# Who rescales the running sums in a graph attention layer: VectorE or GpSimd

## The reference, cut to what matters

```python
q = (h @ Wq + bq).reshape(n, NUM_HEADS, HEAD_DIM) * scaling
k = (h @ Wk + bk).reshape(n, NUM_HEADS, HEAD_DIM)
v = (h @ Wv + bv).reshape(n, NUM_HEADS, HEAD_DIM)
s = jnp.einsum('ehd,ehd->eh', q[row], k[col])
m = jax.ops.segment_max(s, row, num_segments=n)
p = jnp.exp(s - m[row])
denom = jax.ops.segment_sum(p, row, num_segments=n)
attn = p / denom[row]
out = jax.ops.segment_sum(attn[:, :, None] * v[col], row, num_segments=n)
return out.reshape(n, HIDDEN) @ Wo + bo
```

## Time and profile before

| | us |
|---|---|
| median of 3 runs | 8501.01 |
| lowest and highest run | 8488.27, 8502.29 |
| span of the profiled execution | 9608.8 |
| steady part of the changed loop in it | 6100 to 8080 |

### The profile page before, as it was taken

The page is one execution under the profiler, slowest core; times in us unless marked ns, Lnnn a source line. Parts: engine busy times, 40 slices in busy tenths (PEclk is TensorE's granted clock), DMA queues, the critical chain, the costliest instruction groups (busy, mean ns, idle before and its releaser), DMA issues. The chain is left out here.

```text
span 9608.8 us, 121761 instructions
## 1 busy us (share of the span) xinstructions
PE 6035.1 (63%) x27004; PEld 3698.3 (38%) x27227; DVE 5624.6 (59%) x14481; ACT 2416.0 (25%) x7255; POOL 5956.5 (62%) x5564
## 2 busy tenths in 40 slices
PE   2121155555555555547999997899999997554544
PEld 0010033333333333334444444555555555333333
DVE  4100055555555555556888887899999998222224
ACT  0000033333333333322333332344444443000000
POOL 5777655555555555546888884566666665666663
PEclk6555566666666666668999998999999999667676
DMA  1000032223222232322332333344444444333334
GB/s 64 1 10 10 17 88 83 83 78 83 81 80 80 81 83 78 81 55 73 85 84 85 84 84 52 111 120 119 119 119 121 120 119 101 90 90 89 89 90 55
DMA packets 405871, 777.59 MB, mean 81 GB/s; under 512 B 195938, under 2 KB 225356, under 8 KB 405196
## 3 DMA queue, kind: packets, MB, share of 16 engines
q0 software_dynamic: 279488, 712.60, 28.4%
q1 hardware_dynamic: 126348, 64.59, 2.3%
HBM read 736.75 MB, written 40.07 MB: 81 GB/s over the span
## 5 line engine op out<-in xcount | busy, mean ns | idle before, releaser
L495 POOL DMA_INDIRECT rec_s<-wts,rows x784 | 780.5, 995 | 1085.2 <-ACT rows L467 870.5
L1829 POOL DMA_INDIRECT gat<-y,rec_sb_s x892 | 1182.5, 1326 | 298.0 <-issue 278.8
L2098 POOL DMA_INDIRECT gat<-x,rec_sb_d x892 | 846.5, 949 | 484.5 <-issue 266.2
L965 POOL DMA_INDIRECT gat<-kv,rec_sb_d x896 | 906.7, 1012 | 334.7 <-issue 272.9
L1381 POOL DMA_INDIRECT gat<-kv,rec_sb_s x900 | 861.5, 957 | 398.5 <-issue 313.9
L2113 PE MATMUL ps<-gat,oh 128*128 128x256 f32 x1760 | 648.5, 538 | 680.2 <-DVE acc L2133 253.6
L1577 DVE TENSOR_REDUCE small<-ps 128x2 f32<-128x1024 f32 x884 | 1041.7, 1216 | 6.9 <-PE ps L1445 5.7
L434 POOL DMA_INDIRECT rec_d<-small x784 | 810.7, 1034 | 343.0 <-issue 265.1
L1870 PE MATMUL ps<-big,oh 128*128 128x512 f32 x1760 | 947.3, 637 | 0.0
L2113 PEld LDWEIGHTS ps<-gat,oh 128*128 128x128 f32 x1760 | 462.9, 274 | 865.5 <-issue 497.1
L1048 PE MATMUL ps<-big,oh 128*128 128x264 f32 x1768 | 754.1, 541 | 0.3
(11 more groups left out here) (276 smaller groups left out, 13129.7 us busy)
## 6 DMA issues: line engine op xcount, KB each, us to landing
gat<-kv,rec_sb_s POOLq DMA_INDIRECT x900
gat<-kv,rec_sb_d POOLq DMA_INDIRECT x896
rec_sb_s<-rec_s SPq DMA_DIRECT2D x448, 32.0 KB, 2.2
gat<-y,rec_sb_s POOLq DMA_INDIRECT x892
gat<-x,rec_sb_d POOLq DMA_INDIRECT x892
rec_d<-small POOLq DMA_INDIRECT x784
rec_s<-wts,rows POOLq DMA_INDIRECT x784
rec_s<-gat SPq DMA_DIRECT2D x4, 1808.0 KB, 16.7
```

Source lines behind the costliest of these rows:

```text
L495: e.indirect_dma_start(out=recs["s"], out_offset=bass.IndirectOffsetOnAxis(ap=pr[:, t:t + 1], axis=0), in_=rr[:, t, :], in_offset=None).th ...
L965: e.indirect_dma_start(out=gat[:, m.u, q, :], out_offset=None, in_=table, in_offset=bass.IndirectOffsetOnAxis(ap=r_sb[:, m.u, q, 0:1].bitc ...
L1829: e.indirect_dma_start(out=rows_y[m.u][:, q, :], out_offset=None, in_=y1, in_offset=bass.IndirectOffsetOnAxis(ap=r_sb[:, m.u, q, 0:1].bitc ...
L2098: e.indirect_dma_start(out=gat[:, m.u, q, 0:D], out_offset=None, in_=x3, in_offset=bass.IndirectOffsetOnAxis(ap=r_sb[:, m.u, q, 0:1].bitca ...
```

## The change

In the loop of the second attention layer three things move. `rescale` goes from VectorE to GpSimd: in each turn GpSimd first rescales the sums of macro `M(-1)`, then weights the values of `M(0)`, then gathers; it loads the bucket number into a register for that. The first macro has no rescale ahead of it (`pool_first`). The write-back of the running maximum goes from VectorE to ScalarE, as a copy behind the two exponentials, with a bucket load of its own on ScalarE. A new semaphore `kept` counts these copies, and VectorE waits for the copy of the macro before ahead of taking the new maximum. VectorE signals `f` with L1595, and the internal waits that kept L1593 ahead of the write-back are gone. `add_sums` still waits for `rs`, now from GpSimd.

```diff
--- before.py
+++ after.py
@@ -1328,7 +1328,7 @@
         def attention_by_node(table):
 
             s = stages("a2", "far", "oh", "tr", "oht", "qx", "prod", "s3", "st", "sp", "mq", "me", "f", "ef", "p",
-                       "pv", "sum", "rs", "flush")
+                       "pv", "sum", "rs", "flush", "kept")
             s_hm, s_hr = sem("a2_hm"), sem("a2_hr")
             credits.append((s_hr, 3))
             s_rec = [sem(f"a2_rec{u}") for u in range(U)]
@@ -1364,6 +1364,12 @@
             r = recs["s"].rearrange("(p m q) w -> m p (q w)", p=P, q=Q)
 
 
+            def bucket(e, m):
+                return e.value_load(jmap["s"][0:1, bass.ds(m.index(), 1)], min_val=0, max_val=NB - 1)
+
+            def by_head(j):
+                return acc[:, bass.ds(j, 1), :].rearrange("p a (h c) -> p (a h) c", c=HC)
+
             def load_record(e, m):
                 at = e.snap(m.index())
                 e.wait_ge(s["prod"], m.done(U))
@@ -1391,18 +1397,30 @@
                 G.tensor_tensor(pw[:, :, :, 0:DH], gv, pw[:, :, :, DH:HC].to_broadcast([P, Q, H, DH]),
                                 ALU.mult).then_inc(s["pv"], 1)
 
-            def pool_turn(e, M):
+            def rescale(e, m):
+                at = by_head(bucket(e, m))
+                e.wait_ge(s["ef"], m.done())
+                e.wait_ge(s["flush"], m.done(1))
+                G.tensor_tensor(at, at, bcast(ff[m.v], 2, [P, H, HC]), ALU.mult).then_inc(s["rs"], 1)
+
+            def pool_first(e, M):
                 weight_values(e, M(0))
                 gather(e, M(U))
 
+            def pool_turn(e, M):
+                rescale(e, M(-1))
+                weight_values(e, M(0))
+                gather(e, M(U))
+
             def pool(e):
                 G.memset(acc, 0.0).then_inc(S("zeroed"), 1)
-                macro_loops(U, gather, pool_turn, start=1)(e)
+                for m in range(U):
+                    gather(e, Macro(0, m))
+                pool_first(e, lambda lag: Macro(0, lag))
+                macro_loops(0, None, lambda e, M: pool_turn(e, lambda lag: M(1 + lag)))(e)
                 all_landed(e, every_gather)
 
 
-            def bucket(e, m):
-                return e.value_load(jmap["s"][0:1, bass.ds(m.index(), 1)], min_val=0, max_val=NB - 1)
 
             def turn_one_hots(e, m):
                 e.wait_ge(s["oh"], m.done())
@@ -1510,11 +1528,13 @@
                 A.activation(st3[m.v][0:24, :], scores, ACT.Copy).then_inc(s["sp"], 1)
 
             def exponents(e, m):
+                j = bucket(e, m)
                 e.wait_ge(s["f"], m.done())
                 e.wait_ge(s["sum"], m.done(2))
                 A.activation(pvb[:, m.v, :, :].rearrange("p q (h c) -> p q h c", c=HC)[:, :, :, DH],
                              v4(sm), ACT.Exp).then_inc(s["p"], 1)
                 A.activation(ff[m.v], dd, ACT.Exp).then_inc(s["ef"], 1)
+                A.activation(m_run[:, bass.ds(j, 1), :], mn, ACT.Copy).then_inc(s["kept"], 1)
 
             def scalar_turn(e, M):
                 keep_scores(e, M(1))
@@ -1554,15 +1574,6 @@
                 c.wait(k)
                 V.tensor_tensor(t[:, :, 2, :], t[:, :, 1, :], top(t[:, :, 1, :]), ALU.subtract).then_inc(s["s3"], 1)
 
-            def by_head(j):
-                return acc[:, bass.ds(j, 1), :].rearrange("p a (h c) -> p (a h) c", c=HC)
-
-            def rescale(e, m, j):
-                e.wait_ge(s["ef"], m.done())
-                e.wait_ge(s["flush"], m.done(1))
-                V.tensor_tensor(by_head(j), by_head(j), bcast(ff[m.v], 2, [P, H, HC]), ALU.mult)\
-                    .then_inc(s["rs"], 1)
-
             def add_sums(e, m, j):
                 e.wait_ge(s["rs"], m.done())
                 e.wait_ge(s["sum"], m.done())
@@ -1581,20 +1592,17 @@
                 jz = None if start else bucket(e, z)
                 maxima(1)
                 split_scores(c, e, M(1), k_sc)
-                if not start:
-                    rescale(e, z, jz)
                 maxima(2)
                 maxima(3)
                 mj = m_run[:, bass.ds(ja, 1), :]
                 e.wait_ge(s_hr, a.i * (U * PAIRS) + (a.off * PAIRS + PAIRS + 3))
+                e.wait_ge(s["kept"], a.done(1))
                 V.tensor_tensor(mn, mj, mx, ALU.max).then_inc(s["mq"], 1)
                 multiply(e, M(2))
                 e.wait_ge(s["mq"], a.done())
-                k_dd = c(V.tensor_tensor(dd, mj, mn, ALU.subtract))
+                V.tensor_tensor(dd, mj, mn, ALU.subtract)
                 e.wait_ge(s["me"], a.done())
-                c(V.tensor_tensor(v4(sm), s3[a.u][:, :, 0, :], v4(at_edge), ALU.subtract))
-                c.wait(k_dd)
-                V.tensor_scalar(mj, mn, 1.0, None, ALU.mult).then_inc(s["f"], 1)
+                V.tensor_tensor(v4(sm), s3[a.u][:, :, 0, :], v4(at_edge), ALU.subtract).then_inc(s["f"], 1)
                 k_sc = take_scores(c, e, M(2))
                 if not start:
                     add_sums(e, z, jz)
@@ -1617,7 +1625,7 @@
                 multiply(e, Macro(0, 1))
                 k_sc = take_scores(cc, e, Macro(0, 1))
                 vector_turn(cc, e, lambda lag: Macro(0, lag), k_sc, start=True)
-                first, per = cc.n, 4
+                first, per = cc.n, 2
                 e.wait_ge(S("zeroed"), 2)
 
                 def turn(e, M):
```

## The result

Beside the kernel before on one chip, the changed kernel took 8534.94 us (median of 4 runs, 8529.03 to 8538.67) against 8497.3 us (4 runs): ratio 1.0047, 95% interval 1.0035 to 1.0059. That is +38 us where -9 was forecast. The time lies inside the stated range, and it moved the other way; the prediction's chances had leaned to slower (0.34 against 0.28 for faster) while its sum named a gain.

What follows compares the result with a forecast made beforehand. TensorE and VectorE, both 93% busy, were read as two equally long branches before pair 3's reduce. Terms -0.03 - 0.08 + 0.07 = -0.04 us a turn, times 220 = -9 us, gave 8492 us, range 8418 to 8560.

Steps and rivals of the forecast that it cites:

- Rescale on GpSimd: GpSimd's slot between last gather and weighting: 0.63 us rescale after a 0.30 us gap fits, add does not wait.
- Rival B: GpSimd's rescale holds VectorE's difference of maxima, 0.65 us more in 66 turns: +42 us, 8543 us; chance 0.16.
- Rescale off VectorE: Between split and pair 3's reduce: rescale hidden beside TensorE's branch, gain 0.02 to 0.07 us a turn, 0.03 taken.
- Write-back off VectorE: Behind the difference at the edges: the reduce of the products starts sooner, 0.08 us less a turn.
- the new wait: VectorE's wait "kept" ahead of the new maximum: never late, handling costs 0 to 0.09 us a turn, 0.07 taken.
- hidden rescale: VectorE's rescale before pair 3's reduce runs beside an equally long TensorE branch; removal gains 0.03 us a turn.
- A: VectorE sets the pace, so the rescale's 0.35 us a turn comes out in full: -79 us, 8422 us; chance 0.10.
- C: GpSimd's turn becomes the longest, 9.29 us, and the add waits for the rescale: +55 us, 8556; chance 0.16.
- D: TensorE's late release at the edges changes: -83 us (8409), chance 0.07, or +36 us (8528), chance 0.04.

Runs made afterwards that it cites:

- e6: Kernel before plus an idle GpSimd multiply of 128x264 on spare SBUF ahead of each weighting, nobody waiting for it; ratio 1.0076.
- e7: Kernel before plus an idle GpSimd memset of 128x264 on spare SBUF ahead of each weighting; ratio 1.0000.
- e5: Kernel before with the rescale of the running sums left out on every engine; ratio 0.9997.
- e15: Kernel before with only the write-back and its wait moved to ScalarE, rescale left on VectorE, 8494 us chip; ratio 0.9974.
- e9: The whole change, unchanged, run again beside the kernel before on the 9415 us chip; ratio 1.0037.
- e8: Kernel before, unchanged, profiled again on the 9415 us chip; ratio 1.0006.
- e11: Kernel before with only the write-back and its wait moved to ScalarE, rescale left on VectorE, 9415 us chip; ratio 0.9998.
- e0: Kernel before, unchanged, profiled again on the 9602 us chip; ratio 1.0000.

## Why the prediction was wrong, point by point

**The step that failed is "Rescale on GpSimd", in its cost to VectorE.** It checked whether GpSimd has room and whether the add has to wait, found both harmless, and set the instruction at nothing. Both findings hold for the usual turn: the rescale took 0.64 us (0.63 forecast), GpSimd still waited 0.55 us for ScalarE in 204 of 217 turns, and the add waited in 9. But the instruction was costly to an engine that doesn't wait for it: 151 holds of 0.28 us, 42 us in all. Rival B had the mechanism, the place and the sign, at 0.16, and gave 8543 us against 8535 measured. The error was in the weighing. I set it back because no row of before shows a two-input subtract beside a GpSimd multiply. None could: GpSimd had no multiply in that slot before, and in the whole loop none of VectorE's instructions with two SBUF inputs ran beside the weighting. And the sum put the two within 0.02 us of each other.

The Trainium skill, SBUF — State Buffer, states in section Who interferes with whom that a VectorE instruction with two SBUF inputs contends with a GpSimd instruction that reads SBUF, and in section SBUF: two separate sides that the one that starts first keeps the shared ports for its whole length. The runs agree where a GpSimd multiply started first: L1603 ends 0.03 us behind the rescale in all 151 turns (6009.28 and 6009.25 above), and e6 does the same with an idle multiply. Whether a GpSimd instruction that only writes would hold VectorE is barely told by the few turns of e7.

**Rival B's own sum was right by two errors.** It took 0.65 us in 66 turns. Measured: the gap between gather and rescale is 0.02 us, not the 0.30 chosen from gather to gather, so the rescale ends sooner and the hold is 0.28 us where it happens (L1603 0.44 instead of 0.16 us). But it happens in 151 of 221 turns, and on the timed chip L1605 has no wait for TensorE under which a hold could hide. 151 x 0.28 = 42 us, where B had 0.65 x 66 = 43. That its total came within 8 us of the measured time is luck.

**"Rescale off VectorE" was right.** 0.02 to 0.07 us a turn was forecast, 0.03 taken. The wait at pair 3 in after shows it, and the 3 us of e5 are 0.01 a turn, between -0.02 and 0.05 by the interval.

**"Write-back off VectorE" was right in size, the new wait too dear.** After has 0.10 us from L1605 to L1567 (9.21 to 9.31) against 0.19 from L1595 to L1547. The wait "kept" was set at 0.07 us; of the 217 turns 54 pay it, 12.7 us as L1600's wait for L1588, 0.24 us each against the 0.15 that is there anyway: 0.09 x 54 / 217 = 0.02 in the mean. Together -0.07 to -0.10 us a turn on an 8500 us chip, where e15 measured -22 us; the forecast had -0.01.

**What the sum left out: long turns.** Nine times in the loop, in every kernel, GpSimd's second gather of a macro starts 2.02 us behind the end of the first instead of 0.30. Without the rescale on GpSimd its idle time takes that up on an 8500 us chip: in e5 and e15 the turns with such a gather are at most 0.15 us longer than their neighbours of the same place. In after the rescale stands between these gathers and VectorE's add:

```profile
6021.20 0.99 POOL L1387 DMA_INDIRECT gat<-kv,rec_sb_s  x1 [0.80 <-issue]
6024.20 0.95 POOL L1387 DMA_INDIRECT gat<-kv,rec_sb_s  x1 [2.02 <-issue]
...
6027.67 0.64 POOL L1404 TENSOR_TENSOR acc<-acc,small 128x264 f32 x1
```

```profile
6024.94 0.17 DVE L1600 TENSOR_TENSOR small<-m_run,small 128x8 f32<-128x8 f32 x1
...
6028.46 0.43 DVE L1580 TENSOR_TENSOR acc<-acc,ps 128x264 f32 x1 [0.87 <-POOL acc L1404]
...
6035.26 0.58 DVE L1600 TENSOR_TENSOR small<-m_run,small 128x8 f32<-128x8 f32 x1 [0.24 <-DVE small L1588]
```

That turn is 6035.26 - 6024.94 = 10.32 us. Four of the nine are of this kind, where the loop closes, and five take 9.54 us in the third place. Against e5's turns in the same places (8.67 and 8.58) that is 4 x 1.65 + 5 x 0.96 = 11 us, 0.05 a turn. L1603 is not held in them. I looked at mean slack (rows of a usual turn) where the rare gap decides. The row was there to be read, in the waits of before behind the earlier trace rows:

```profile
POOL gat L1381 <- issue: 305.8, 770, 2.0
```

The last line of VectorE's above has something else that no forecast had: L1600, the new maximum, took 0.58 us instead of 0.17, beside a gather. It does so behind the four turns of 10.3 us, in after as in e9, and ends 0.06 us behind that gather. Its cause stays open.

**The balance for the 8497 us chip,** by turn against a kernel before of about 8.61 (e5 8.601, e7 8.620, both with ratio 1.000): hold +0.19, long turns +0.05, write-back with its wait -0.07 to -0.10, hidden rescale -0.01: +0.13 to +0.16, times 220 = 29 to 35 us. Turn measured: 8.775 - 8.61 = +0.165, 36 us. Time measured: +38. That the kernel before would have had a turn of 8.61 there is an estimate, and a few us stay unexplained.

**The other rivals.** A (VectorE sets the pace) falls with e5. C (GpSimd's turn the longest) falls as a state of every turn and is seen in nine of them. D names something real, a release that comes late on some chips (0.54 us in 153 turns on the 9600 us kind, 47 turns in a stretch of e8 on the 9415 us chip, none in after's steady stretch on the 8497 us chip). On the timed chip it has no part in the loss. On the slow ones it is there in every kernel, but its count moves with the kernel: over the whole loop of the 9415 us chip 51 turns in e8, 104 in e9, 76 in e11.

## What to carry to other kernels

Before an instruction is given to GpSimd, look at what VectorE does in that very slot: a small VectorE subtract with both inputs in SBUF was held for the rest of a GpSimd multiply, and it is the slot, not the engine, that made the difference between +38 and -24 us (all of those 24 are the write-back's). Making the multiply wait until VectorE was past the slot cured the hold and won nothing, since its result then came late. Look for holds in mean durations, since they show as busy time. And ask first whether the instruction to be moved is on the path: here two branches of equal length ran side by side, and leaving the instruction out altogether gained 3 us, no more than noise.

## What the runs showed of the hardware

- A VectorE TENSOR_TENSOR of 128x8 with two SBUF inputs grew from 0.15 to 0.44 us when it started in the middle of a GpSimd TENSOR_TENSOR, and ended 0.03 us behind it (after, 151 turns). When it started in the last 0.08 us of it, it kept 0.16 us (50 turns). In the seven turns of e7 in which a memset had more than 0.1 us left it kept 0.155 us.
- Beside indirect gathers most of VectorE's instructions with two SBUF inputs kept their lengths (the rescale on VectorE, 0.433 us in 118 turns of before). The new maximum did not always: 0.22 to 0.24 us instead of 0.17 in 92 turns of before, and 0.58 us in four turns of after and four of e9.
- GpSimd's multiply follows an indirect gather at 0.02 us, while gathers follow each other at 0.30 and a gather follows a multiply at 0.80 us. In after its address load (0.29 us) ran while a gather was busy and cost nothing visible.
- About every 26 turns (227 us in after) one gather starts 1.7 us late, nine times in the loop, in all kernels. Why is not known.
- The same kernel took 8494 to 9602 us in five comparisons, 13% apart. VectorE's wait for TensorE's maxima at the edges came in 153 of 221 turns (e0, 9602 us), in 51 (e8, 9415 us) and in one (e5, 8506 us). The cause stays open.
